# Clamping the squared norms of keys and queries after the root instead of before it, and on VectorE instead of ScalarE

## The reference

```
q = causal_conv_silu(x @ Wq.T, conv_q); k = ...(Wk, conv_k); v = ...(Wv, conv_v)     # 4 taps
q = q / max(sqrt(sum(q*q)), 1e-6); k = k / max(sqrt(sum(k*k)), 1e-6)                  # per head
alpha = exp(-exp(A_log) * softplus(x @ Wa.T + dt_bias)); beta = 2 * sigmoid(x @ Wb.T)
for each t:  S = alpha * (S - beta * k (k S)) + k v;   o = S q
attention = rms_norm(o) @ Wo.T
```

## Time and profile before

| quantity | value |
|---|---|
| median of 3 runs | 4922.19 us (4921.31 to 4924.02) |
| the profiled execution's own time | 4922.06 us |
| its span | 4920.1 us |
| TensorE matmuls busy | 89% of the span |
| VectorE | 73% |
| ScalarE | 58% |
| GpSimd | 27% |
| mean share of the 16 DMA engines | about 18% in the loop |

### The profile page before, as it was taken

The page is one execution under the profiler, slowest core; times in us unless marked ns, Lnnn a source line. Parts: engine busy times, 40 slices in busy tenths (PEclk is TensorE's granted clock), DMA queues, the critical chain, the costliest instruction groups (busy, mean ns, idle before and its releaser), DMA issues. The chain is left out here.

```text
span 4920.1 us, 155226 instructions
## 1 busy us (share of the span) xinstructions
PE 4354.5 (89%) x59788; PEld 3200.6 (65%) x59788; DVE 3584.4 (73%) x8216; ACT 2863.4 (58%) x4519; POOL 1311.9 (27%) x1318
## 2 busy tenths in 40 slices
PE   5999999999999999999899999989999998999955
PEld 4666666666666666666666666666666666666644
DVE  6777777777777777777777777777777777777745
ACT  2555656565565656555565655556565655656533
POOL 2222222222222222222222222222222222222211
PEclk9999999999999999999999999999999999999977
DMA  1111111111111111111111111111111111111111
GB/s 51 43 38 41 36 38 40 36 41 38 41 36 39 39 36 41 38 41 36 42 36 36 41 38 41 36 42 36 36 40 38 41 37 41 36 36 40 36 36 42
DMA packets 873889, 191.75 MB, mean 39 GB/s; under 512 B 811904, under 2 KB 869504, under 8 KB 873856
## 3 DMA queue, kind: packets, MB, share of 16 engines
q1 hardware_dynamic: 867552, 173.48, 16.7%
q0 software_dynamic: 6304, 17.84, 1.3%
HBM read 136.16 MB, written 55.06 MB: 39 GB/s over the span
## 5 line engine op out<-in xcount | busy, mean ns | idle before, releaser
L803 DVE SCALAR_TENSOR_TENSOR cv<-ps,w_v,cv 128x512 f32<-128x512 f32 x768 | 576.7, 751 | 382.3 <-ACT cv L669 364.2
L803 DVE SCALAR_TENSOR_TENSOR cv<-ps,w_kq,cv 128x512 f32<-128x512 f32 x768 | 574.3, 748 | 85.7 <-ACT cv L669 67.6
L525 PEld LDWEIGHTS ps<-Z,NM 64*64 64x64 f32 x8192 | 263.0, 135 | 330.2 <-issue 330.2
L585 PE MATMUL ps<-QG,S 64*128 64x64 f32 x4096 | 431.8, 274 | 4.1
L588 PE MATMUL ps<-PT,U 64*128 64x64 f32 x4096 | 429.3, 272 | 0.0
L978 POOL TENSOR_TENSOR qn<-sl,sq 128x512 f32<-128x512 f32 x128 | 161.9, 1265 | 980.6 <-ACT sq L707 980.6
L445 PE MATMUL ps<-Lm,k_all 128*128 128x512 f32 x768 | 418.4, 626 | 0.0
L525 PE MATMUL ps<-Z,NM 64*64 64x64 f32 x8192 | 294.3, 221 | 132.3 <-DVE accT L915 132.3
L669 ACT ACTIVATE cv<-ps,w_kq 128x512 f32<-128x512 f32 x256 | 175.9, 687 | 398.4 <-PE ps L434 398.4
L585 PEld LDWEIGHTS ps<-QG,S 64*128 64x128 f32 x4096 | 342.6, 188 | 31.4 <-issue 31.4
L963 POOL COPY stP<-tabP 128x24 f32 (+1 forms) x128 | 25.3, 197 | 1220.0 <-DVE KT L832 1213.0
(11 more groups left out here) (177 smaller groups left out, 10306.6 us busy)
## 6 DMA issues: line engine op xcount, KB each, us to landing
scrN<-Nd SPq DMA_DIRECT2D x256, 128.0 KB, 2.4
Z<-scrZ SPq DMA_DIRECT2D x256, 128.0 KB, 2.8
X<-scrX SPq DMA_DIRECT2D x256, 128.0 KB, 3.0
w_v<-wtab SPq DMA_DIRECT2D x128, 132.0 KB, 2.5
w_kq<-wtab POOLq DMA_DIRECT2D x128, 132.0 KB, 2.4
wo_s<-wo SPq DMA_DIRECT2D x128, 128.0 KB, 2.4
NS<-scrN SPq DMA_DIRECT2D x128, 64.0 KB, 2.5
scrZ<-XT SPq DMA_DIRECT2D x128, 64.0 KB, 2.5
```

What stands on the lines that cost most here:

```text
L525: last = nc.tensor.matmul(sub_block(ps, 2 * 512, b, a, z), sub_block(BD["NM"], 0, b, a, z), sub_block(BD["Z"], 0, b, a, z), start=True, st ...
L585: nc.tensor.matmul(o_cols(h, b), unit(S, b)[a:z], sub_block(BD["QG"], 0, b, a, z), start=True, stop=False)
L803: nc.vector.scalar_tensor_tensor(cv4[:, j], pj[:, :, k:k + C], tap(j, k), cv4[:, j], ALU.mult, ALU.add).then_inc(conv.sem, 1)
```

## The change

The clamp is moved. Before, ScalarE formed max(s - 1e-12, 0), and then Ln(that + 1e-12), from the squared norm s. After, Ln(s + 1e-19) is taken directly from PSUM, and the factor exp(-0.5 * Ln) is clamped from above at 1e6 where it is used, in one `scalar_tensor_tensor` (min with 1e6, then multiply) on VectorE. This takes the place of `tensor_tensor` for the keys. For the queries it is a new instruction on VectorE, `dve_queries`, behind sub 9, and GpSimd's product is gone. The signal `nrm_mx` is now given by Ln, at Ln's place in the order.

```
-        def act_norm_max(act, n, i):
+        def act_norm_ln(act, n, i):
             act.wait_ge(nrm_mm.sem, nrm_mm.at(n, i + 1))
-            nc.scalar.activation(half(sq, i), bank((4, 6)[i]), ACT.Relu, bias=eps[:, 3:4]).then_inc(nrm_mx.sem, 1)
-
-        def act_norm_ln(act, n, i):
+            nc.scalar.activation(half(sq, i), bank((4, 6)[i]), ACT.Ln, bias=eps[:, 2:3]).then_inc(nrm_mx.sem, 1)
+
+        def act_norm(act, n, i):
             act.wait_ge(nrm_mx.sem, nrm_mx.at(n, i + 1))
-            nc.scalar.activation(half(sq, i), half(sq, i), ACT.Ln, bias=eps[:, 2:3]).then_inc(nrm_ln.sem, 1)
-
-        def act_norm(act, n, i):
-            act.wait_ge(nrm_ln.sem, nrm_ln.at(n, i + 1))
             nc.scalar.activation(half(sq, i), half(sq, i), ACT.Exp, scale=-0.5).then_inc(nrm_rn.sem, 1)
...
@@ act_body
                 act_tap0(act, n, 1)
-                act_norm_max(act, n, 0)
...
                 act_norm(act, n, 0)
-                act_norm_max(act, n, 1)
...
@@ dve_keys
-            nc.vector.tensor_tensor(half(BD["KB"], 0), half(sl, 0), half(sq, 0), ALU.mult).then_inc(kb_ok.sem, 1)
+            nc.vector.scalar_tensor_tensor(half(BD["KB"], 0), half(sq, 0), 1.0 / EPS_L2, half(sl, 0), ALU.min, ALU.mult).then_inc(kb_ok.sem, 1)
+
+        def dve_queries(dve, n):
+            dve.wait_ge(nrm_rn.sem, nrm_rn.at(n, 2))
+            if not first(n):
+                dve.wait_ge(gram_p.sem, gram_p.at(n - 1))
+                dve.wait_ge(qg_ok.sem, qg_ok.at(n - 1))
+            nc.vector.scalar_tensor_tensor(qn[:], half(sq, 1), 1.0 / EPS_L2, half(sl, 1), ALU.min, ALU.mult).then_inc(qn_ok.sem, 1)
...
@@ dve_body
                 dve_sub(dve, n, 0, 10)
+                dve_queries(dve, n)
...
@@ pool_prepare
-            pool.wait_ge(nrm_rn.sem, nrm_rn.at(n, 2))
-            if not first(n):
-                pool.wait_ge(gram_p.sem, gram_p.at(n - 1))
-            nc.gpsimd.tensor_tensor(qn[:], half(sl, 1), half(sq, 1), ALU.mult).then_inc(qn_ok.sem, 1)
```

More of the change, by code:

```diff
@@ L41 @@
 EPS_L2 = 1e-6
+LN_FLOOR = 1e-19
 EPS_RMS = 1e-6
@@ L196, in _ @@
                 nc.gpsimd.memset(eps[:, 1:2], EPS_RMS).then_inc(zeroed.sem, 1)
-                nc.gpsimd.memset(eps[:, 2:3], EPS_L2 * EPS_L2).then_inc(zeroed.sem, 1)
-                nc.gpsimd.memset(eps[:, 3:4], -EPS_L2 * EPS_L2).then_inc(zeroed.sem, 1)
+                nc.gpsimd.memset(eps[:, 2:3], LN_FLOOR).then_inc(zeroed.sem, 1)
+                nc.gpsimd.memset(eps[:, 3:4], 0.0).then_inc(zeroed.sem, 1)
                 nc.gpsimd.memset(xnT3[:, :, 0:HALO], 0.0).then_inc(zeroed.sem, 1)
@@ L351, in build @@
         nrm_mx = sig("nrm_mx", 2)
-        nrm_ln = sig("nrm_ln", 2)
         nrm_rn = sig("nrm_rn", 2)
```

## The result

The changed kernel takes 5272.02 us (median of 4 runs, 5259.88 to 5280.54) against 4921.94 us before (4921.31 to 4924.02): ratio 1.0709, interval 1.0687 to 1.0730. The forecast was 5299 us in 5190 to 5400 us. The profiled execution took 5280.54 us, with a span of 5278.8 us.

What follows compares the result with a forecast made beforehand. The pass was taken as bound by VectorE up to convolution 1, then TensorE from z(0). Wait 2.76, less 0.41 saved, plus 0.62 for the clock gave 2.97 us a pass; over 127 passes 4922 + 377 = 5299 us, range 5190 to 5400.

Steps and rivals of the forecast that it cites:

- The wait: On TensorE, z(0) waits for the keys' Ln to free bank 4, starting at 2428.74 instead of 2425.98: +2.76 us a pass.
- a pass without a fall: Loop pass, Nd to Nd, in which TensorE's clock does not drop to half: forecast 35.49 + 2.76 - 0.62 = 37.6 us.
- Relu, keys: Two Relu passes removed from ScalarE, and KB by scalar_tensor_tensor within its slack on VectorE: both counted as 0.
- Queries and holds: VectorE up to KT: new instruction +0.63, sub 11 held +0.23, two GpSimd holds gone -0.88 and -0.95: -0.97 us.
- convolution 0 waited for tap 0: VectorE's convolution 0 held by tap 0, so only 0.62 us of 0.97 arrives; mean 0.41, none in passes with a fall.
- The clock: TensorE's new idle before z(0) drops its clock to half in one pass of two, at 1.25 us each: +0.62 us a pass.
- the old falls: Half-clock stretches of TensorE in 43 of 127 present passes, 15.4 to 16.1 us behind Nd, costing 0.87 to 1.07 us each.
- the wait alone: Rival: z(0) waits for Ln, no new falls of the clock; 2.35 us a pass, 5220 us; chance 0.20.
- A fall in every pass: Rival: TensorE's clock falls behind z(0) in each pass; 3.60 us a pass, 5379 us; chance 0.16.
- "faster" rival: Rival: z(0) does not wait for Ln, only GpSimd's untangling is left, 52 us saved, 4870 us; chance 0.04.

Runs made afterwards that it cites:

- e2: Kernel before with only the keys' half of the change (Ln from PSUM, min and product on VectorE), queries as before: 5463.68 us, ratio 1.1098.
- e1: Changed kernel with the keys' Relu, Ln from SBUF and tensor_tensor put back, so only the queries' half remains: 4889.86 us, ratio 0.9937.
- e3: Changed kernel with the first round of z in free PSUM bank 5, so z(0) does not wait for the keys' Ln: 4886.97 us, ratio 0.9932.
- e5: Kernel before with one move on GpSimd, NM ahead of the queries' product qn: 4874.12 us, ratio 0.9908.
- e4: Changed kernel with two added unused 128x512 matmuls ahead of z(0)'s waits, the wait for Ln kept: 5134.72 us, ratio 1.0434.
- e6: Kernel before with one added unused 128x512 matmul in the idle ahead of the transposition of KB: 4878.86 us, ratio 0.9923.
- e8: Changed kernel with z(0) in bank 5 and one added unused matmul ahead of the transposition of the values: 4801.91 us, ratio 0.9766.

## Why the prediction was right

*The wait.* The step that carried the forecast was z(0) at Ln's end. Priced at 2.76 us less 0.62 us, a pass without a fall was to take 37.6 us; it takes 37.63. e2 shows the first number alone (38.22 - 35.5 = 2.7 us), e1 the second (35.5 - 34.92 = 0.6 us), and e3 takes the wait out and gets all of it back. z(0) started 0.17 us behind Ln, not 0.24.

*Relu, keys.* Both at nothing, as forecast: e5 keeps both Relus, e1 the keys' alone and e3 neither, and their undisturbed passes are equal; e1 and e3 differ in `KB` too.

*Queries and holds.* 0.69 us for the instruction (0.63 us with the overlap), within 0.01 us of the price. Sub 11 was held as foreseen: it took 0.40 us instead of 0.25, 0.15 us where 0.23 were priced. From `Nd` to `KT` VectorE needs 1.09 us less, where 0.97 were priced (2417.25 - 2399.00 before, 17.16 us after). And convolution 0 waited for tap 0 (0.88 us idle before it), so that not all of it arrived: 0.60 of the 0.62 us forecast.

*The clock.* Here the price of a fall, the number of falls and the fate of the old ones were all off, and the total came near by luck, since the errors cancel in part. I put 0.62 us on top of the present falls, as one new fall in two passes at 1.25 us each. Measured, 78 of 126 passes have one, 75 of them at 1.5 to 1.7 us, at the upper bound given (1.67); by the means, 38.63 - 37.63 = 1.00 us a pass. But the old falls, 35.86 - 35.51 = 0.35 us a pass, are gone: all stretches of the changed kernel lie around z(0) or behind it. Net +0.65 us. The prediction also took 0.21 us off the saving for passes with an old fall, of which there are none any more. Those 0.2 us are the difference between 2.97 us a pass forecast and 38.63 - 35.86 = 2.77 us measured: 127 x 0.2 = 25 us of the 27 us by which the forecast was too high. Why the old falls vanish is not settled. e3 has the same idle times before its transpositions as the changed kernel, and falls there in 54 of its passes. It lacks the idle before z(0), but neither that idle nor the falls behind it can be what keeps the old ones away: e4 fills the one for the most part and is rid of the others, and the old falls stay away all the same (3 of 126). The late z(0) and the longer pass are what e4 and the changed kernel share against e3.

The rivals: the wait alone (5220 us, with the old falls) can be compared with e4, 5134.72 us with neither old nor new ones, plus 127 x 0.35 = 44 us for the old: 5179 us. The difference is the 0.21 us a pass named above and z(0)'s start. A fall in every pass did not come, nor did a gain, though e3 shows that the gain of the "faster" rival is real once the wait is gone (4887 us against 4870). It is smaller than priced because the clock falls in more passes of the shorter length, 54 against 43, and by the means 35.86 - 35.59 = 0.27 us a pass are saved instead of 0.41.

One reading was a little off: the old stretches start 15.3 to 16.3 us behind `Nd`, not 15.4 to 16.1. Nothing in the sum hangs on it.

## What to carry to other kernels

When two passes of an engine are fused, look at what the first of them released. A cheap copy, placed early, may be what frees a PSUM bank, and the fused instruction gives it back where the later one stood, here behind a Silu and a table load, with z(0) 2.7 us later for 0.7 us of work saved on an engine that waited anyway. And look at what a two-operand instruction on VectorE meets on GpSimd: one product moved in GpSimd's order was worth 0.9% (e5).

## What the runs showed of the hardware

A short idle of TensorE can cost more than its length: with 2.64 us of idle before z(0), 75 of 126 passes lost another 1.5 to 1.7 us at half clock (three more lost 2.2 to 3.2 us), and in e2 74 passes lost 2.7 to 2.9 us. Unused matmuls in the idle left the undisturbed pass as long as it was and took nearly all falls away: e4 is 137 us faster by them (some 14 of it z(0)'s earlier start), e6 39 us against the kernel's own run on that chip (4918.08 us), e8 85 us against e3. But an idle need not bring falls: 1.6 us before the transposition of the values had 54 falls beside it in e3, 3 in e4 and none in the changed kernel. A 64x2 instruction on VectorE took 1.05 us beside a GpSimd `tensor_tensor` and 0.16 us without, and it ended within 0.03 us of GpSimd's end. The new `scalar_tensor_tensor` from two SBUF inputs was held likewise: 0.69 us free, as in the pass of the changed kernel above, and 1.08 us when it started during GpSimd's product of the decays in e3:

```profile
2413.19 1.27 POOL L976 TENSOR_TENSOR ex<-ex,k_all 128x512 f32<-128x512 f32 x1
...
2413.93 1.08 DVE L804 SCALAR_TENSOR_TENSOR KB<-sq,sl 128x512 f32<-128x512 f32 x1
```

GpSimd ends at 2414.46, and `KB` 0.55 us later, so all but 0.14 us of its 0.69 us lie behind GpSimd's end. That agrees with the exclusive lock that the Trainium skill (SBUF — State Buffer, § SBUF: two separate sides) states for an instruction with two SBUF inputs, and which the trace of before could show for `tensor_tensor` only.
